# Softplus in the scan of a Mamba-style block: one ScalarE function in place of three passes and a VectorE step

## What is computed

```python
dts = jnp.einsum('bkrl,kdr->bkdl', dts, dt_proj_w)
delta = jax.nn.softplus(dts + dt_proj_b[None, :, :, None])
A = -jnp.exp(A_logs).reshape(K, D_INNER, D_STATE)
def step(h, inp):
    ul, dl, Bl, Cl = inp
    dA = jnp.exp(dl[..., None] * A)
    h = dA * h + (dl * ul)[..., None] * Bl[:, :, None, :]
    y = jnp.einsum('bkdn,bkn->bkd', h, Cl)
    return (h, y)
```

## Time and profile before

| | us |
|---|---|
| median of 3 executions | 13929.23 |
| lowest and highest | 13920.08 and 13971.47 |
| the profiled execution, its own time | 13937.71 |
| span of its profile | 13935.9 |

### The profile page before, as it was taken

How to read it: one execution, slowest core, us unless ns; L and a number is a source line. 1 busy time by engine, 2 the same in 40 slices (tenths; PEclk the granted TensorE clock), 3 DMA queues, 4 the chain that set the end, 5 groups by cost and what they waited for, 6 DMA issues and landing times. The chain is left out here.

```text
span 13935.9 us, 133740 instructions
## 1 busy us (share of the span) xinstructions
PE 10742.2 (77%) x41528; PEld 4591.2 (33%) x41528; DVE 12036.7 (86%) x8096; ACT 6887.5 (49%) x9171; POOL 10348.0 (74%) x4494
## 2 busy tenths in 40 slices
PE   8877777777777777777777777777777759999999
PEld 5522222222222222222222222222222237777778
DVE  7699999999999999999999999999999955555554
ACT  4355555555555555555555555555555533444443
POOL 1199889989998998999899999998899962222220
PEclk9866766666666666776677667766666768999999
DMA  3333332333333333333332333333333331111110
GB/s 105 112 102 113 113 122 101 105 118 120 108 105 109 124 108 111 118 104 111 116 121 101 110 115 124 103 103 113 123 111 107 109 90 37 41 40 37 37 37 10
DMA packets 371594, 1357.09 MB, mean 97 GB/s; under 512 B 47080, under 2 KB 47784, under 8 KB 367566
## 3 DMA queue, kind: packets, MB, share of 16 engines
q1 hardware_dynamic: 370894, 1348.53, 29.9%
HBM read 983.45 MB, written 364.90 MB: 97 GB/s over the span
## 5 line engine op out<-in xcount | busy, mean ns | idle before, releaser
L803 POOL TENSOR_TENSOR HC<-H,crep 128x1024 f32<-128x1024 f32 x3072 | 7227.9, 2365 | 989.9 <-DVE H L660 974.2
L553 PE MATMUL psum<-sx,selb 96*128 96x512 f32 x5888 | 3003.7, 610 | 2257.0 <-DVE H L660 1578.4
L660 DVE TENSOR_TENSOR_SCAN H<-E,car,psum 128x1024 f32<-128x1024 f32 x1728 | 4055.6, 2347 | 61.6
L553 PEld LDWEIGHTS psum<-sx,selb 96*128 96x128 f32 x5888 | 1296.9, 268 | 5496.1 <-issue 4553.1
L589 PE MATMUL psum<-HC,sely 128*32 128x512 f32 x12288 | 3080.9, 845 | 12.1 <-POOL HC L803 12.1
L640 DVE TENSOR_TENSOR psum<-dur,psum 128x1024 f32<-128x1024 f32 x2304 | 2784.0, 1208 | 230.4 <-PE psum L553 230.4
L735 ACT ACTIVATE E<-dlr,am 128x1024 f32<-128x1024 f32 x2304 | 2626.5, 1145 | 348.7 <-DVE H L660 347.3
L735 ACT ACTIVATE psum<-dlr,am 128x1024 f32<-128x1024 f32 x768 | 858.6, 1118 | 1971.5 <-DVE H L660 1963.3
L795 POOL TENSOR_TENSOR dbu<-dur,brep 128x1024 f32<-128x1024 f32 x768 | 1814.0, 2362 | 0.0
L741 ACT COPY car<-H 128x1 f32<-128x1 f32 x2304 | 425.7, 185 | 2117.8 <-DVE H L660 2111.1
L660 DVE TENSOR_TENSOR_SCAN H<-psum,car,dbu 128x1024 f32<-128x1024 f32 x576 | 1320.0, 2333 | 96.1 <-POOL dbu L795 93.1
(11 more groups left out here) (127 smaller groups left out, 10005.9 us busy)
## 6 DMA issues: line engine op xcount, KB each, us to landing
dur<-scr_dlu SPq DMA_DIRECT2D x768, 512.0 KB, 4.5
dlr<-scr_dl SPq DMA_DIRECT2D x768, 512.0 KB, 7.1
scr_dl<-dlt SPq DMA_DIRECT2D x256, 384.0 KB, 3.0
scr_dlu<-dlu SPq DMA_DIRECT2D x256, 384.0 KB, 3.0
scr_yk<-yt SPq DMA_DIRECT2D x256, 384.0 KB, 3.4
yp<-scr_yk SPq DMA_DIRECT2D x128, 384.0 KB, 8.9
scr_xa<-xs SPq DMA_DIRECT2D x64, 384.0 KB, 3.5
scr_sz<-xs SPq DMA_DIRECT2D x64, 384.0 KB, 3.5
```

The source lines that it names most:

```text
L553: r = e.matmul(o[:, sub * 512:(sub + 1) * 512], selb[:, which, :], sx[:, c % 2, sub * 512:(sub + 1) * 512], start=True, stop=True)
L660: e.tensor_tensor_scan(H[:, un % NH, ::step], decay[:, ::step], drive[:, ::step], init, ALU.mult, ALU.add).then_inc(scan_done)
L803: e.tensor_tensor(HC[:, un % NHC, :], H[:, un % NH, :], crep[:, g, :], ALU.mult).then_inc(hc_done)
```

## The change

ACT's `delta` becomes one activation with the function Softplus from PSUM straight into `dl`, with the bias `dtb`. DVE's `delta` is gone, and with it `ndtb`, `c20`, their setup and the semaphore `softplus`.

```diff
@@ def vector
-        def delta(m):
-            b, k, ci, half = steps[m]
-            kk = k * 2 + half
-            e.wait_ge(softplus, 3 * (m + 1))
-            if m:
-                e.wait_ge(dl_out, 16 * m)
-                e.wait_ge(dlu_made, m)
-            e.scalar_tensor_tensor(dl, stage[0:C, :], dtb[:, kk:kk + 1], dlu[:], ALU.add, ALU.max).then_inc(dl_made)
...
-        delta(0)
-        delta(1)
...
-                if n % 2 and x == 0:
-                    delta(n + 1)
-                if n % 2 and x == 6:
-                    delta(n + 2)
@@ def scalar
             e.wait_ge(dt_done, m + 1)
             if m:
-                e.wait_ge(dlu_out, 16 * m)
-            e.activation(dlu[:], stage[0:C, :], ACT.Relu, bias=ndtb[:, kk:kk + 1], scale=-1.0).then_inc(softplus)
-            e.wait_ge(softplus, 3 * m + 1)
-            e.activation(dlu[:], dlu[:], ACT.Exp, bias=c20[:], scale=-1.0).then_inc(softplus)
-            e.wait_ge(softplus, 3 * m + 2)
-            e.activation(dlu[:], dlu[:], ACT.Ln, bias=1.0).then_inc(softplus)
+                e.wait_ge(dl_out, 16 * m)
+                e.wait_ge(dlu_made, m)
+            e.activation(dl, stage[0:C, :], ACT.Softplus, bias=dtb[:, kk:kk + 1]).then_inc(dl_made)
...
-        e.preload_act_table_set("natural_log_exp_and_others")
+        e.preload_act_table_set("exp_and_others")
@@ def pool
             e.wait_ge(dl_made, m + 1)
+            if m:
+                e.wait_ge(dlu_out, 16 * m)
             e.wait_ge(u_in, 32 * (b + 1))
```

More of the change, by code:

```diff
@@ L310, in scan_phase @@
     dtb = T("dtb", [C, NK * 2])
-    ndtb = T("ndtb", [C, NK * 2])
-    c20 = T("c20", [C, 1])
     am = T("am", [128, NK * 2 * NJ * NG])
@@ L359, in scan_phase @@
     dt_done = sem("dt_done")
-    softplus = sem("softplus_step")
     dl_made = sem("dl_made")
@@ L594, in tensor @@
         e.wait_ge(consts_in, NCONST)
-        e.wait_ge(ve_set, 3)
+        e.wait_ge(ve_set, 1)
         project(0, 0)
@@ L664, in vector @@
         e.tensor_copy(selb[:], selbf).then_inc(ve_set)
-        e.memset(c20[:], 20.0).then_inc(ve_set)
-        e.tensor_scalar(ndtb[:], dtb[:], -1.0, 20.0, ALU.mult, ALU.add).then_inc(ve_set)
         e.tensor_reduce(dsum[:], ds[:], AX.X, ALU.add).then_inc(skip_made)
@@ L679, in vector @@
             scan(un)
-            if c < NCHUNK:
-                if n % 2 == 0 and x == 8:
-                    split(c)
-                if n % 2 and x == 0:
-                    delta(n + 1)
-                if n % 2 and x == 6:
-                    delta(n + 2)
+            if c < NCHUNK and n % 2 == 0 and x == 8:
+                split(c)
     def scalar(e):
```

## The result

The changed kernel took 14014.67 us (median of 20, 13952.42 to 14047.95) against 13945.91 us (median of 20) for the kernel before. The ratio, taken over all executions, is 1.0036, with a 95% interval from 1.0021 to 1.0051: slower by some 50 us (the means are 51.5 us apart, the medians 68.8), within the half per cent that counts as no change, and clear of zero. The forecast was 13953 against a median of 13929.23, +23.5 us or 1.0017, so its sign and case came true and its size was less than half the measured one. The profiled execution took 14031.01 us, its span is 14029.2 us, 93.3 us over that of before.

What follows compares the result with a forecast made beforehand. DVE was taken to set the scan's pace, POOL close behind, with waits for `yp` and `dbu` absorbing savings. Terms -75.5 - 6 + 105 = +23.5 us gave 13953 against 13929.23, called same; range 13845 to 14070.

Steps and rivals of the forecast that it cites:

- DVE's step: Scan: removing 256 softplus steps of 1.18 us gains 75.5 us in directions 0 and 1, none in 2 and 3.
- The second comes off a stretch in which POOL is the bound: Scan, directions 0 and 1: removing the second softplus step only lengthens DVE's wait for `dbu`, 1.89 to 3.07 us.
- in directions 2 and 3 ... starts again at the same moment: Scan: DVE's wait on late `yp` grows from 3.06 to 5.42 us, so removing both steps gains 0.
- ACT's block: Scan: two table loads and Softplus take 3.67 us, 0.4 more than before; hidden with 1.9 us to spare, cost 0.
- The rival of dearer loads: Scan and post phase: each table load costs twice its row; sum +175 us, 14105 us; chance 0.05.
- The start of the scan: Before the scan is running, nothing hides ACT's passes: two in a chain, some 3 us each less one load, -6 us.
- The loads behind the scan: Post phase: Ln and Exp each need a table load, 185 us of ACT, of which +105 with 5 for clock.
- each pair of loads costs its whole 2.57 us: Image 0's layer norm: tiles follow in a ring of ACT and DVE, 5.80 us growing to 8.37; 21 us in all.
- the statistics' pair there ends in slack: Post phase, images 1 to 7: the two table loads at the statistics add nothing to the time.
- PE's longer gaps may cost it clock ... I add 5 us: Post phase: longer PE gaps may lower its granted clock, 0.91 behind the scan; 5 us added.
- The rival of full price in the post phase: Post phase: nothing absorbs the pairs of table loads, +103 us, 14033 us; chance 0.25.
- The whole saving on DVE: Scan: DVE's waits shrink with its removed steps, so all 302 us arrive; sum -203 us, 13726 us; chance 0.10.

Runs made afterwards that it cites:

- experiment 4: Changed kernel with the table set named, plus a DVE reduction of constants in odd half steps: ratio 0.9996 at unit 0, 0.9954 at unit 6.
- experiment 3: SP issues the load of `yp` earlier: ratio 0.9815 on the changed kernel with the table set named, 0.9898 on the kernel before.
- e5_dve_unit0: Changed kernel with the table set named, plus a DVE reduction of constants at unit 0 of odd half steps: ratio 0.9996.

## Why the prediction was right, and where its size was off

*DVE's step.* Its price of 1.18 us, the wait behind which each half of the saving would go, and its worth by direction stand. "The second comes off a stretch in which POOL is the bound" is what experiment 4 shows, and "in directions 2 and 3 ... starts again at the same moment" what experiment 3 shows. The term itself, -75.5, came out at -60.8 in the profiled pair. Four profiles have the scan of the kernel before (10593.4 to 10610.5 us) and three that of the changed one (10517.8 to 10543.8); the means are 72 us apart. Nearly all that differs lies in the odd half steps, and their sum by direction, each from its first recurrence to that of the next half step (so without the very last), shows which directions pay:

```text
                               directions 0 and 1   directions 2 and 3
scan as before (4 profiles)     2705.9 to 2706.4     2790.6 to 2809.3
single Softplus (3)             2630.4 to 2630.8     2791.6 to 2817.0
scan as before, yp ahead (1)    2706.2               2665.8
single Softplus, yp ahead (3)   2630.4 to 2631.0     2590.6 to 2591.2
reduction at unit 0 (1)         2688.6               2794.2
reduction at unit 6 (1)         2630.4               2787.3
Softplus four times (1)         2741.7               2797.8
```

In directions 0 and 1 the gain is 75.5 us, as forecast to a tenth. In 2 and 3 it is 0 as forecast, with up to 25 us between executions of one and the same scan, which is where the profiled pair's 61 comes from; with `yp` ahead it is 75 there too. The reduction at unit 0 and the longer block on ACT are paid in directions 0 and 1 alone (58 and 111 us).

*ACT's block.* Forecast 0, measured 1.5 us of waiting in all, at the start of the scan. Softplus at 1.11 us and the load at 1.28 were both as taken. The Trainium skill (ScalarE: Activation LUTs, What ACT_TABLE_LOAD costs) adds a drain of 1380 ns to each load; the trace shows 4.7, 4.5, 1.2 and 1.1 us of idle time before the 638 loads of the four groups above, 0.02 us each, and in the rows above the activation begins 0.02 us behind its load. The rival of dearer loads is gone with that.

*The start of the scan.* -9.7 against -6: the first load, which I had counted as exposed (1.28 us), fell into ACT's wait for PE, and the second pass no longer waits for `dlu` to go out, which had held it 1.7 us. The rest, 0.9 us, lies ahead of the first pass.

*The loads behind the scan.* That they would come, from the rows of the pre phase, was the step that mattered; without it the forecast had been 13848. Their size, +105 with 5 for clock, measured about 98, but made up otherwise. Image 0 was forecast at +2.57 us a tile, 8.37 us apart and 21 us in all; its tiles are 6.81 us apart, 1.01 more than before, and the image pays some 11 us (rows of the changed kernel, answering to the earlier trace rows):

```profile
11283.88 0.68 ACT L1305 ACTIVATE rs<-psum,eps 96x512 f32<-96x512 f32 x1
...
11290.69 0.68 ACT L1305 ACTIVATE rs<-psum,eps 96x512 f32<-96x512 f32 x1
```

The step that failed there is "each pair of loads costs its whole 2.57 us". The rows show why in DVE's scaling, two instructions that the ring waits for. Before, they ran beside a product of POOL's and took 2.98 us; the loads push them behind it, and they take 1.29 us, which gives back 1.69 of the 2.57. First DVE and POOL before, then after:

```profile
11352.97 2.98 DVE L1202 TENSOR_TENSOR y<-y,rs 96x512 f32<-96x512 f32 x2 [1.63 <-ACT rs L1329]
11352.46 2.95 POOL L1420 TENSOR_TENSOR y<-y,szt 96x512 f32<-96x512 f32 x2
```

```profile
11286.53 1.29 DVE L1180 TENSOR_TENSOR y<-y,rs 96x512 f32<-96x512 f32 x2 [3.69 <-ACT rs L1307]
11283.32 2.48 POOL L1398 TENSOR_TENSOR y<-y,szt 96x512 f32<-96x512 f32 x2
```

In images 1 to 7 the ring grew from 8.57 to 11.27 us (forecast 11.14), and PE's wait for the Ln from the earlier trace rows to 104.1 us:

```profile
11443.90 0.68 ACT L1305 ACTIVATE rs<-psum,eps 96x512 f32<-96x512 f32 x1
...
11455.17 0.68 ACT L1305 ACTIVATE rs<-psum,eps 96x512 f32<-96x512 f32 x1
```

```profile
PE psum L1080 <- ACT rs L1305: 104.1, 17, 9.3
```

In the profiled pair an image gained 8.5 to 12.6 us (forecast 11.3), and some 20 us in two images in which PE's wait for the statistics doubled (from 7.9 to 14.9 us and from 7.7 to 15.7). That is no sign against "the statistics' pair there ends in slack": in the second profile of the changed kernel the two waits were 7.1 and 6.1 us and those images gained as little as the others, while a kernel without loads had 13.9 (e5_dve_unit0). What lengthens that wait in some executions stays open.

*Where the size was off.* The term "PE's longer gaps may cost it clock ... I add 5 us" was mis-sized, as far as the profiles can tell. In the profiled pair two more images closed at the low clock, some 57 us. By the means of the profiles the other terms give -72 for the scan, -8 for its start and +98 for the loads, +18 us; the measured difference over 20 executions each is some 50. The 30 us between them are the length of one slow image more in an execution. The slow images of those executions were not counted, so this is an inference, and so is the part that the loads have in it.

*The rivals.* The rival of full price in the post phase was forecast at 14033 us, close to the 14031.01 of the profiled execution, but not for its reason: of 185 us of loads about 100 landed, with clock on top. The whole saving on DVE did not arrive: it would have been 302 us, and 72 came. The loads came.

## What to carry to other kernels

A table set that one phase loads serves every phase behind it: changing it there moves loads into code that the diff doesn't touch, so name the set at the head of each phase (0.9% here, 0.7% of it the loads themselves), and look for pairs of functions that only a combined set serves. The Trainium skill's rule to use the combined set for Exp and Ln (ScalarE: Activation LUTs, Rules for kernel authors) holds with that number beside it. Before work is taken off the busiest engine, look for the wait behind which it will vanish; here one issue of a DMA, moved ahead of others in its queue, was worth more (139 us on the kernel before) than the change in the scan (72), and doubled what the change was worth there: both together, with the set named, gave 0.9815 and 0.9796 of the time before.

## What I had not expected

PE's closing matmuls of one image take 34.9 us or about 63.6 at the same code, the clock staying at 1.00 or, behind the first few of them, at 0.50 with PE busy throughout, and which images do changes from one execution to the next. None to four slow images, at 28.7 us each, could make most of the spread of this kernel between executions (13914 to 14047 us), and two of them outweigh the effect measured here; profiles of two kernels can only be compared behind the scan after counting slow images. And a delay of 2.57 us on one engine cost only 1.01 us in image 0, it seems because it took apart two instructions each of DVE and POOL: 2.98 to 1.29 us and 2.95 to 2.48 us. The Trainium skill (SBUF — State Buffer, Who interferes with whom) has a DVE instruction with two SBUF inputs contend with a GpSimd instruction that reads SBUF. These rows agree, but no run took the pair apart by itself.
